# Sums over partitions in bursts of four groups, two bursts behind, with a product ring of twelve and a weight ring of eight

## The reference, cut to what matters

```python
vi = x[:, i_idx, :]                          # x: 512 x 40 x 64, the looked-up rows
vj = x[:, j_idx, :]
viW = jnp.einsum('bpd,pde->bpe', vi, W)      # W: 780 x 64 x 64
out = jnp.einsum('bpe,bpe->bp', viW, vj)     # 512 x 780
```

## Time and profile before

| | before |
|---|---|
| median of 3 runs | 349.3 us (348.85 to 350.2) |
| profiled execution, its own time | 349.04 us |
| its span in the trace | 346.9 us |
| granted PE clock over the span | 0.995 |
| PE busy | 329.1 us (95%) |
| DVE busy | 249.6 us (72%) |
| POOL busy | 225.6 us (65%) |
| ACT busy | 22.1 us (6%) |

### The profile page before, as it was taken

The page is one execution under the profiler, slowest core; times in us unless marked ns, Lnnn a source line. Parts: engine busy times, 40 slices in busy tenths (PEclk is TensorE's granted clock), DMA queues, the critical chain, the costliest instruction groups (busy, mean ns, idle before and its releaser), DMA issues.

```text
span 346.9 us, 4306 instructions
## 1 busy us (share of the span) xinstructions
PE 329.1 (95%) x1676; PEld 115.1 (33%) x1676; DVE 249.6 (72%) x248; ACT 22.1 (6%) x35; POOL 225.6 (65%) x191
## 2 busy tenths in 40 slices
PE   0799979899999999999999999999999999999997
PEld 0133333233333333333333333333333333333442
DVE  2484968778787888978889888988888898840000
ACT  1001100000000000000001000010000000000032
POOL 6777777777778889877788788576887423520000
PEclk9999989999999999999999999999999999999999
DMA  6984443243423238731322323232110000000000
GB/s 167 255 231 146 119 106 105 81 102 91 115 57 104 64 96 261 170 104 33 96 85 62 89 68 86 62 69 85 39 23 2 0 3 0 0 2 0 0 2 0
DMA packets 17854, 27.59 MB, mean 80 GB/s; under 512 B 4901, under 2 KB 5029, under 8 KB 17834
## 3 DMA queue, kind: packets, MB, share of 16 engines
q1 hardware_dynamic: 9770, 17.86, 17.7%
q0 software_dynamic: 4608, 4.73, 6.9%
q10 hardware_dynamic: 3456, 4.72, 4.8%
HBM read 22.57 MB, written 0.00 MB: 65 GB/s over the span
## 4 chain that ended last, share of the span: by engine, by line
PE 80%; POOL 13%; issue 4%; DMA 1%; ACT 0%
PE ps_t L421 47%; PE ps_z L443 21%; POOL rows L265 13%; PE ps_t L465 5%; PE ps_e L404 2%; PE ps_t L488 2%; PE ps_e L465 2%; DMA rows<-in_tbl,ids_sb 1%; DMA ids_sb<-in_ids_t 1%; PE ps_t L494 1%; ACT y_sb L328 0%
## 5 line engine op out<-in xcount | busy, mean ns | idle before, releaser
L372 DVE TENSOR_TENSOR prod<-ps_t,E 128x1024 f32<-128x1024 f32 x200 | 231.7, 1217 | 45.7 <-PE ps_t L421 44.9
L421 PE MATMUL ps_t<-E,w_sb 64*128 64x512 f32 x800 | 189.8, 609 | 0.8 <-ACT E L294 0.7
L265 POOL DMA_INDIRECT rows<-in_tbl,ids_sb x144 | 137.8, 957 | 43.4 <-issue 41.9
L272 POOL TENSOR_TENSOR prod<-prod 128x1024 f32<-128x1024 f32 x37 | 86.8, 2370 | 37.4 <-DVE prod L372 37.3
L421 PEld LDWEIGHTS ps_t<-E,w_sb 64*128 64x128 f32 x800 | 71.1, 187 | 109.6 <-issue 82.2
L443 PE MATMUL ps_z<-prod,quads 128*32 128x512 f32 x572 | 76.8, 600 | 0.0
L443 PEld LDWEIGHTS ps_z<-prod,quads 128*32 128x32 f32 x572 | 15.1, 109 | 48.9 <-DVE prod L372 29.1
L351 DVE TENSOR_SCALAR prod<-prod,first_row_f 125x512 f32<-125x512 int32 x38 | 16.6, 495 | 11.1 <-PE ps_e L395 5.1
L294 ACT ACTIVATE E<-ps_e 128x512 f32<-128x512 f32 x18 | 10.8, 598 | 192.4 <-PE ps_e L404 171.1
L395 PE MATMUL ps_e<-prod 125*64 125x512 f32 x40 | 12.1, 694 | 11.2 <-DVE prod L351 10.0
L465 PE MATMUL ps_t<-z,w_sb 128*128 128x512 f32 (+1 forms) x42 | 18.6, 595 | 0.0
(11 more groups left out here) (26 smaller groups left out, 21.1 us busy)
## 6 DMA issues: line engine op xcount, KB each, us to landing
w_sb<-in_w_units SPq DMA_DIRECT2D x50, 256.0 KB, 2.9
E<-E ACTq DMA_DIRECT2D x72, 64.0 KB, 2.3
rows<-in_tbl,ids_sb POOLq DMA_INDIRECT x144, 2.6
w_sb<-in_w SPq DMA_DIRECT2D x7, 256.0 KB, 4.5
prod<-in_ids_by_field SPq DMA_DIRECT2D x2, 512.0 KB, 9.0
prod<-in_tbl SPq DMA_DIRECT2D x3, 312.5 KB
w_sb<-in_w SPq DMA_DIRECT2D x1, 512.0 KB, 7.1
prod<-in_tbl SPq DMA_DIRECT2D x1, 250.0 KB
```

The lines of the kernel that those rows point to most:

```text
L265: pool.indirect_dma_start(rows[:, g % G_RING, b, f * DIM:(f + 1) * DIM], None, tables[2 * k + f], bass.IndirectOffsetOnAxis(ap=ids_sb[:, c ...
L272: pool.tensor_tensor(prod[:, n % P_RING, 0, :, :], prod[:, n % P_RING, 0, :, :], prod[:, n % P_RING, 1, :, :], ALU.add).then_inc(halves_ad ...
L372: dve.tensor_tensor(prod[:, n % P_RING, s, :, :], ps_t[:, (2 * n + s) % STEPS, :, :], multiplier, ALU.mult).then_inc(product_ready, 1)
L421: last = pe.matmul(ps_t[:, step % STEPS, j, :], w_sb[at:at + DIM, m % W_RING, col:col + P], E[at:at + DIM, slot_of(pairs_of(n)[s][j]), :], ...
```

## The change

The sums are taken for four groups (two units) in one go, after every fourth group: `TOGETHER` = 4, and `LAG` now counts such bursts and is 2. `reduce(r)` takes the sums of groups 4r to 4r+3 after the products of group 4r+11. The product ring grows from 8 to 12 groups, the weight ring shrinks from 12 to 8 units. The list of groups whose halves POOL adds is written out, and has 34 groups in place of 37: groups 34, 62 and 98 are no longer added. (A way to add halves by DMA is there too, and no group uses it.) `E4` loses an entry that nothing used. The tail after the loop is written anew.

```diff
-W_RING = 12
-P_RING = 8
+W_RING = 8
+P_RING = 12
 STEPS = 3
-LAG = 7
+TOGETHER = 4
+LAG = 2
...
-ADDED = [n for n, (_, M) in enumerate(GROUPS) if M is not None and n >= 20 and n // 2 % 2 == 1]
+ADDER = "...........P.P.P...P.P.P.P.P.P...P.P.P.P.P.P.P.P.."
+ADDED_BY_POOL = [n for n in range(NG) if ADDER[n // 2] == "P"]
...
             def multiply(n):
                 k, M = GROUPS[n]
                 if n >= P_RING:
-                    dve.wait_ge(two_reduced, (n - P_RING) // 2 + 1)
+                    dve.wait_ge(reduced, (n - P_RING) // TOGETHER + 1)
...
-            def reduce_two(n):
-                c, q = divmod(n // 2, PER_CHUNK // 2)
-                if c >= 1 and q == 0:
+            def reduce(r):
+
+                c, at = divmod(r * TOGETHER // 2, PER_CHUNK // 2)
+                if c >= 1 and at == 0:
                     pe.wait_ge(z_copied, c)
-                for g in (n, n + 1):
-                    pe.wait_ge(product_ready, 2 * g + 2)
...
+                for q in range(at, at + TOGETHER // 2):
+                    n = c * PER_CHUNK + 2 * q
                     for g in (n, n + 1):
+                        pe.wait_ge(product_ready, 2 * g + 2)
...
-                last.then_inc(two_reduced, 1)
+                last.then_inc(reduced, 1)
...
                 else:
                     products(at)
-                    if at >= LAG and at % 2 == 1:
-                        reduce_two(at - LAG)
+                    if (at + 1) % TOGETHER == 0 and (at + 1) // TOGETHER > LAG:
+                        reduce((at + 1) // TOGETHER - LAG - 1)
...
-            reduce_two(NG - 6)
             pe.wait_ge(params_loaded, 16 * (CHUNKS + 5))
             pe.wait_ge(z_copied, CHUNKS - 2)
             pe.wait_ge(e_copied, KP)
             sum_h1(0, 0, CHUNKS - 2)
-            reduce_two(NG - 4)
-            sum_h1(0, CHUNKS - 2, CHUNKS - 1)
+            reduce(NR - 2)
             pe.wait_ge(product_ready, 2 * NG - 2)
-            sum_h1(1, 0, CHUNKS - 1)
-            reduce_two(NG - 2)
-            for m in range(2, H1 // P):
-                sum_h1(m, 0, CHUNKS - 1)
+            sum_h1(1, 0, CHUNKS - 2)
+            sum_h1(2, 0, CHUNKS - 2)
+            pe.wait_ge(z_copied, CHUNKS - 1)
+            reduce(NR - 1)
+            pe.wait_ge(product_ready, 2 * NG - 1)
+            sum_h1(3, 0, CHUNKS - 2)
+            for m in range(H1 // P):
+                sum_h1(m, CHUNKS - 2, CHUNKS - 1)
```

More of the change, by code:

```diff
@@ L60 @@
 CHUNKS = -(-NG // PER_CHUNK)
+NR = NG // TOGETHER
 LAST_ROWS = 2 * (NG - PER_CHUNK * (CHUNKS - 1))
 DENSE_AT = 32 * (BLOCKS - 1) + LAST_ROWS
-ADDED = [n for n, (_, M) in enumerate(GROUPS) if M is not None and n >= 20 and n // 2 % 2 == 1]
+ADDER = "...........P.P.P...P.P.P.P.P.P...P.P.P.P.P.P.P.P.."
+ADDED_BY_POOL = [n for n in range(NG) if ADDER[n // 2] == "P"]
+ADDED_BY_DMA = [n for n in range(NG) if ADDER[n // 2] == "D"]
+ADDED = sorted(ADDED_BY_POOL + ADDED_BY_DMA)
 def arrival(k):
@@ L133, in tower_kernel @@
         E = sb("E", [P, E_RING, BATCH])
-        E4 = sb("E4", [P, QUADS, 2, BATCH])
+        E4 = sb("E4", [P, QUADS - 1, 2, BATCH])
         w_sb = sb("w_sb", [P, W_RING, BLOCKS * P])
@@ L189, in tower_kernel @@
         halves_added = sem("halves_added")
-        two_reduced = sem("two_reduced")
+        halves_added_by_dma = [sem(f"halves_added_by_dma{i}") for i in range(P_RING)]
+        reduced = sem("reduced")
         z_copied = sem("z_copied")
@@ L271, in add_halves @@
                 pool.wait_ge(product_ready, 2 * n + 2)
+                if n in ADDED_BY_DMA:
+                    pool.dma_start(prod[:, n % P_RING, 0, :, :], prod[:, n % P_RING, 1, :, :],
+                                   accum_op=ALU.add).then_inc(halves_added_by_dma[n % P_RING], 16)
+                    return
                 pool.tensor_tensor(prod[:, n % P_RING, 0, :, :], prod[:, n % P_RING, 0, :, :],
@@ L300, in copy_fields @@
                         to, of = (2 * (k % 2) + f) * HALF, f * DIM + h * HALF
-                        act.dma_start(E4[to:to + HALF, k // 2, h, :], E[of:of + HALF, slot_of(k), :]).then_inc(
+                        act.dma_start(E4[to:to + HALF, k // 2 - 1, h, :], E[of:of + HALF, slot_of(k), :]).then_inc(
                             e4_placed[u], 16)
             def copy_z(c):
-                act.wait_ge(two_reduced, PER_CHUNK // 2 * (c + 1))
+                act.wait_ge(reduced, PER_CHUNK // TOGETHER * (c + 1))
                 act.activation(z[:, c, :], ps_z[:], ACT.Copy).then_inc(z_copied, 1)
@@ L313, in _ @@
                         copy_fields(at)
-                elif at % 2 == 1 and at > LAG and (at - LAG + 2) % PER_CHUNK == 0:
-                    copy_z((at - LAG) // PER_CHUNK)
+                elif (at + 1) % TOGETHER == 0:
+                    done = (at + 1) // TOGETHER - LAG
+                    if done > 0 and done % (PER_CHUNK // TOGETHER) == 0:
+                        copy_z(done // (PER_CHUNK // TOGETHER) - 1)
             copy_z(CHUNKS - 2)
-            act.wait_ge(two_reduced, NU)
+            act.wait_ge(reduced, NR)
             top = 32 * (BLOCKS - 1)
@@ L365, in multiply @@
                     if M is not None:
-                        multiplier = E4[:, M, s, None, :].to_broadcast([P, 2, BATCH])
+                        multiplier = E4[:, M - 1, s, None, :].to_broadcast([P, 2, BATCH])
                     elif s == 0:
@@ L378, in _ @@
                 multiply(n)
-            dve.wait_ge(two_reduced, NU)
+            dve.wait_ge(reduced, NR)
             top = 32 * (BLOCKS - 1)
@@ L423, in products @@
                     last.then_inc(step_done, 1)
-            def reduce_two(n):
-                c, q = divmod(n // 2, PER_CHUNK // 2)
-                if c >= 1 and q == 0:
+            def reduce(r):
+                c, at = divmod(r * TOGETHER // 2, PER_CHUNK // 2)
+                if c >= 1 and at == 0:
                     pe.wait_ge(z_copied, c)
-                for g in (n, n + 1):
-                    pe.wait_ge(product_ready, 2 * g + 2)
-                    if g in ADDED:
-                        pe.wait_ge(halves_added, ADDED.index(g) + 1)
-                for s in range(2):
-                    for g in (n, n + 1):
[L435 to L446, removed]
-                last.then_inc(two_reduced, 1)
@@ new lines, in reduce @@
+                for q in range(at, at + TOGETHER // 2):
+                    n = c * PER_CHUNK + 2 * q
+                    for g in (n, n + 1):
+                        pe.wait_ge(product_ready, 2 * g + 2)
+                        if g in ADDED_BY_POOL:
+                            pe.wait_ge(halves_added, ADDED_BY_POOL.index(g) + 1)
+                        elif g in ADDED_BY_DMA:
+                            pe.wait_ge(halves_added_by_dma[g % P_RING],
+                                       16 * sum(a % P_RING == g % P_RING for a in ADDED_BY_DMA if a <= g))
+                    for s in range(2):
+                        for g in (n, n + 1):
+                            if s == 1 and g in ADDED:
+                                continue
+                            if GROUPS[g][1] is None:
+                                ones = halves[:, 30 - 4 * q - 2 * s:62 - 4 * q - 2 * s]
+                            else:
+                                ones = quads[:, 28 - 4 * q:60 - 4 * q]
+                            for j in range(2):
+                                to = 32 * (2 * (g % 2) + j)
+                                last = pe.matmul(ps_z[to:to + 32, :], ones, prod[:, g % P_RING, s, j, :],
+                                                 start=(q == 0 and s == 0),
+                                                 stop=((q == PER_CHUNK // 2 - 1 or n == NG - 2)
+                                                       and (s == 1 or g in ADDED)))
```

## The result

| | before | after |
|---|---|---|
| median | 349.53 us (348.85 to 350.2, 4 runs) | 364.27 us (363.61 to 366.3, 4 runs) |
| profiled execution, span | 349.04, 346.9 us | 364.14, 362.1 us |

The ratio is 1.0431, with a 95% interval of 1.0385 to 1.0478: slower by 4.3%. The forecast was 365.0 us, range 360.5 to 368.5. The slowest of the four (366.3 us) also has the lowest mean granted clock, 0.986 against 0.991 to 0.995; where its clock fell isn't shown, since it has no trace.

The account below looks back on a forecast made before the run. Prediction: POOL's gathers bound the kernel up to about 66 us, then PE alone. To 349.04 us it added -4.2 (changes, start, tail), +23.3 (waits), -4.9 (transpositions), +1.6 (clock): 364.8, median 365.0, range 360.5 to 368.5.

Parts of the forecast that it names:

- The stretch of eight steps: PE's products of four groups in the loop: 8.12 us with waits for DVE from step 4, 7.06 without.
- waits of +23.3 us: PE's waits for DVE in the loop's 22 long stretches, 1.06 us each.
- The first rival: At step 4 of each stretch PE doesn't wait: stretches 7.06 us, total 344.8 or 346.4 us; chance 0.04.
- Bursts and tail: Sums in the loop take 2.71 or 3.57 us; after the loop, the second layer starts at 351.6 us.
- Transpositions: In the loop, three before stretches cost 0.6 us each, nine before step 2 or 6 lose 0.24 each; together 4.0.
- The start: Up to 68.27 us: PE idles 3.6 us before the transposition at 65.76; group 11 ends at 68.27 as before.
- a fall of the clock: Behind PE's gap before the transposition at 65.76 us, the clock falls and adds 1.6 us.
- The sign that I had named: PE's gap before 65.76 us starts from 62 on, with a clock under 1.00 behind it.
- The other rivals: Short pauses in the loop's stretches make the clock fall repeatedly, 400 or 374 us, chance 0.05; late adds, rows or weights, 0.05.
- No add, row or weight tile came late: Rival: after 70 us PE waits for POOL or a DMA, total 366 to 370 us; chance 0.05.
- The rings: Weight tiles issued 8 units ahead in place of 12 cost nothing; only a landing of over 40 us would show.

Follow-up runs that it names:

- e1: Changed kernel, DVE multiplying only the first three quarters of each step's columns from group 12 on: 345.83 us, ratio 0.9893 to the kernel before.
- e2: Kernel before, DVE multiplying only the first three quarters of each step's columns from group 8 on: 349.82 us, ratio 0.9994.
- b1: Kernel before, with eight transpositions after group 16 moved one group forward, between sums and products: 348.64 us, ratio 0.9968.
- e3: Kernel before with only sizes changed: weight ring 8, product ring 12, groups 34, 62 and 98 not added by POOL: 349.76 us, ratio 0.9999.
- e4: Changed kernel with sums of one unit at a time again, but as late as in the change: 354.17 us, ratio 1.0110 to the kernel before.
- b3: Kernel before with eight transpositions moved forward, POOL's adds rearranged, and the third unit's sums moved into PE's gap before 66 us: 343.82 us, ratio 0.9823.
- e5: Changed kernel with only its first burst moved from behind group 11 to behind group 7: 362.41 us, ratio 1.0352 to the kernel before.

## Why the prediction was right

*The stretch of eight steps.* Forecast 8.12 us, measured 8.11 to 8.14. This is the largest term of the forecast (waits of +23.3 us in a sum of +15.8), and its mechanism is shown twice: by the starts of PE's steps, and by e1 and e2, in which DVE's pace alone is changed. The first rival's condition (0.86 us a multiply) was made in e1, and its time came: 345.83 us against 344.8 to 346.4.

*Bursts and tail.* Forecast 2.71 and 3.57 us, measured 2.71 and 3.57; from the last burst of the loop to the second layer 33.53 us (317.56 to 351.09), forecast 2.71 + 30.8.

*Transpositions.* Those before step 2 and step 6 cost 0.24 us each, as forecast (stretches of 8.35, once 8.38). One stretch, from 287.21 to 295.91, took 0.35 us more: DVE's third multiply started late there. It is the place at which b1 lost 0.3, and the kernel before has a late multiply there too (277.17, 1.60 us behind 275.57), hidden.

*The start.* Here the sum was right only in total, and that is luck: two errors of opposite sign, -1.6 and +0.73 us, partly cancel. I had put the idle time of PE in one gap of 3.6 us ahead of the transposition near 66, and a fall of the clock behind it on the path, 1.6 us. In fact the gathers ran later (the transposition that I put at 55.8 stood at 57.10) and the products ahead of it were done earlier (53.73), so the larger gap (3.37 us) came there, the clock fell in the groups behind that one, and the second gap swallowed it: 0 in place of 1.6. The sign that I had named, a clock under 1.00 behind the last gap, didn't come. Against that the last gather landed later than before, and group 11 ended at 69.00 in place of 68.27: +0.73. The prediction took that time over from the trace of before as if it were fixed; in the traces of this study the transposition stands anywhere from 65.8 to 67.3, in kernels with either order.

*The balance.* The second layer was forecast 15.8 us later and came 15.28 later (351.09 against 335.81): 15.8 - 1.6 + 0.73 + 0.35 = 15.28. The 0.35 us is the late multiply, which no term of the forecast had.

*The other rivals.* In the trace the clock fell once, at the start, and in 248.56 us of stretches with short pauses not at all (1.00), so such pauses of 0.2 to 0.3 us don't make it swing here. The second failure mode that the Trainium skill describes (TensorE: Matmul & The Clock Gate, A second HAM failure mode: psum-queue depth-cycling) doesn't appear in this trace. No add, row or weight tile came late behind 69 us. The rings did nothing (e3), as costed.

*The parts.* The lateness of the sums costs about 4 us (e4, 353.6 to 354.2). The long stretches cost 22 x 1.06 less what they save; without DVE's pace the change won 3.9 us by the medians (e1).

## What to carry to other kernels

Fewer switches of a producer are a gain only as long as the buffer between it and its consumer covers the longer run: count how far the slower consumer falls behind in one run (here 0.27 us a step, three places) and find the first step that has to wait. Of the lengths that ran here only four steps in a row end before that point; six lose 0.5 us (b3) and eight 1.06. PE's sums are the time in which DVE catches up. Look at distances between starts, not at busy shares, for pauses shorter than an instruction's row; and before moving work to a later place, see what gap it filled at the old one. Before moving it to an earlier place, see what will set the time then: in e5 and b3 PE met POOL's gathers again at a later transposition.

## What the runs showed of the hardware

Float32 work of one shape is very regular on PE: 35 or 36 stretches of 16 records take 3.63 us each in four of these kernels (before, e2, e3, e4), to a nanosecond or two. Around an early gap of PE the granted clock was at its lower level (1.2 GHz) for 3.4 us, once (e4) for 6.8, but where that began differed from trace to trace: with the first instruction behind a gap of 2.15 us in the kernel before, 1.1 us after it (58.21 against 57.10) in the changed one, and in e3 1.2 us behind its gap of 1.88 us; three traces (e2, b1, b3) show no fall there at all. What a fall costs depends on what PE waits for next: behind the last gap it cost 1.6 us (e3) and 2.7 us (e4), and where PE had to wait for rows later on it cost nothing (the changed kernel, e5). It is likely part of the spread between executions of one kernel, which wasn't tested.

The gathers that the same program sends at the start don't land at the same time: the transposition near 66 us started between 65.76 and 67.32 in the traces in which PE waited for its rows.
